# State sums of a decayed linear attention with the values as weights, and a transpose behind them

## The reference, cut to what matters

```python
Q = _xpos((x @ Wq).reshape(B, T, H, 128), 1.0)
K = _xpos((x @ Wk).reshape(B, T, H, 128), -1.0)
V = (x @ Wv).reshape(B, T, H, 64)
scores = jnp.einsum('bihd,bjhd->bhij', Q, K) * DQK ** (-0.5)
scores = scores * _decay_mask(T)[None]      # causal decay, rows normalised
out = jnp.einsum('bhij,bjhv->bihv', scores, V)
... # group norm over time, a silu gate, Wo, residual; then the feed-forward part
```

## Time and profile before

| | us |
|---|---|
| median of 3 runs | 905.84 |
| lowest and highest | 901.13, 906.43 |
| the profiled execution | 905.14 |
| its span, first to last instruction | 903.3 |
| TensorE busy in it | 858.9 |

### The profile page before, as it was taken

One profiled execution on the slowest core, in us unless ns is written; L12 is line 12 of the kernel. 1 busy time (PEld: TensorE's weight loads), 2 busy tenths in 40 slices (PEclk: granted clock), 3 DMA queues, 4 the chain that ended last, 5 costly groups with the idle time before them and its releaser, 6 DMA issues.

```text
span 903.3 us, 16221 instructions
## 1 busy us (share of the span) xinstructions
PE 858.9 (95%) x5414; PEld 399.1 (44%) x5414; DVE 657.6 (73%) x1608; ACT 588.4 (65%) x891; POOL 527.9 (58%) x481
## 2 busy tenths in 40 slices
PE   8799999999999989889899999999999999999997
PEld 3477777777688756222222222322232223222222
DVE  5666656665476687958688888878888887877774
ACT  2232322345442356868689898889979897988784
POOL 0456555544365624566857576758675767575552
PEclk9999999999999999899999999999999999999998
DMA  9500002000000097768588989788988888989773
GB/s 266 221 1 1 2 1 75 1 1 1 1 2 13 18 156 176 241 190 260 170 262 236 277 233 289 235 282 235 282 236 277 252 275 230 280 257 301 250 247 102
DMA packets 90110, 154.28 MB, mean 171 GB/s; under 512 B 30326, under 2 KB 56374, under 8 KB 89635
## 3 DMA queue, kind: packets, MB, share of 16 engines
q1 hardware_dynamic: 89542, 151.63, 55.6%
q10 hardware_dynamic: 486, 1.62, 1.2%
HBM read 138.96 MB, written 15.83 MB: 171 GB/s over the span
## 4 chain that ended last, share of the span: by engine, by line
PE 75%; ACT 10%; DVE 7%; issue 4%; POOL 2%; DMA 1%; ACTq 0%; DVEq 0%; POOLq 0%; SPq 0%
PE ps L876 17%; PE ps L813 16%; PE ps L496 5%; PE ps L852 5%; PE ps L519 3%; PE ps L590 3%; PE ps L504 3%; PE ps L643 3%; PE ps L599 3%; ACT ring L1202 2%; PE ps L529 2%; PE ps L561 2%; PE ps L581 2%; PE ps L612 2%; PE ps L664 1%
## 5 line engine op out<-in xcount | busy, mean ns | idle before, releaser
L1885 POOL TENSOR_TENSOR ring<-ring,wbc 128x512 f32<-128x512 f32 x192 | 245.0, 1278 | 151.7 <-ACT ring L1211 142.3
L1668 DVE TENSOR_TENSOR ring<-ps,ring 128x1024 f32<-128x1024 f32 x192 | 234.6, 1222 | 82.3 <-PE ps L852 55.7
L813 PE MATMUL ps<-zst,w1st 99*128 99x512 bf16 x768 | 210.9, 384 | 12.3 <-ACT ring L1202 7.3
L876 PE MATMUL ps<-ring,w2cur 128*32 128x512 f32 x1536 | 206.6, 611 | 0.0
L1202 ACT ACTIVATE ring<-ps 128x1024 f32<-128x1024 f32 x192 | 196.9, 1026 | 3.9 <-PE ps L813 3.8
L1213 ACT ACTIVATE ps<-ps 128x512 f32<-128x512 f32 x192 | 113.3, 590 | 56.5 <-PE ps L813 56.3
L1671 DVE TENSOR_TENSOR ring<-ps,wbc 128x512 f32<-128x512 f32 x192 | 130.8, 681 | 0.2 <-DMA wbc<-w_rows 0.2
L813 PEld LDWEIGHTS ps<-zst,w1st 99*128 99x128 bf16 x768 | 60.7, 97 | 137.1 <-issue 37.3
L1211 ACT ACTIVATE ring<-ps 128x512 f32<-128x512 f32 x192 | 116.6, 607 | 0.0
L1734 POOL TENSOR_TENSOR s2q<-s2q,rope 128x768 f32<-128x768 f32 x24 | 43.1, 1817 | 91.0 <-ACT s2q L1014 91.0
L852 PEld LDWEIGHTS ps<-wst,sel 32*128 32x128 bf16 x384 | 18.1, 91 | 150.7 <-DVE ring L1668 95.9
(11 more groups left out here) (181 smaller groups left out, 1297.7 us busy)
## 6 DMA issues: line engine op xcount, KB each, us to landing
wbc<-w_rows SPq DMA_DIRECT2D x192, 512.0 KB, 5.3
w2cur<-in_w SPq DMA_DIRECT2D x48, 256.0 KB, 4.9
w_parts<-wp SPq DMA_DIRECT2D x72, 64.0 KB, 3.1
zst<-z_parts SPq DMA_DIRECT2D x72, 64.0 KB, 4.3
wst<-w_parts SPq DMA_DIRECT2D x24, 128.0 KB, 4.0
z_parts<-zp SPq DMA_DIRECT2D x6, 384.0 KB, 6.3
wst<-w_parts SPq DMA_DIRECT2D x24, 96.0 KB, 3.8
out_h<-h SPq DMA_DIRECT2D x12, 192.0 KB, 5.4
```

Source lines behind the costliest of these rows:

```text
L813: return pe.matmul(bank(to), w1st[0:99, 4 * a + j, col:col + P], zst[0:99, (i // 2) % 2, j, :], start=True, stop=True)
L876: mm = pe.matmul(bank(YBANK, 0, 512, 32 * j, 32 * j + 32), w2cur[:, n, j, :], ring[:, (4 * g + j) % RING, :], start=False, stop=(n == 7 an ...
L1668: dve.tensor_tensor(v, ps[:, WBANK * 512:WBANK * 512 + 1024], v, ALU.mult).then_inc(s["duo_done"], 1)
L1885: pool.tensor_tensor(ring[:, slot, :], ring[:, slot, :], wbc[:, g % 4, 1, :], ALU.mult).then_inc(s["tri_done"], 1)
```

## The change

It concerns pairs 0 to 4 (`flips(k)`), that is the first five chunks of batches 0 and 1. Pairs 6 to 10 keep the old way.

- `flipped_sums` takes vn (64 columns) as weights and t1k (128 columns) as what moves. There are as many matmuls as before, 12 for each pair, and two heads go to the two column halves. The result is the transposed state: partitions are two heads by 64 values, columns the 128 query-key places, for three groups of heads.
- `add_sums` keeps this transposed state in buffer 0, in place: one instruction of 384 columns for x = 0, two (128 and 256 columns) for x = 1, whose sums lie in three banks.
- `turn_state` is new on TensorE: six transposes of 128 x 128 in the trip after the one that makes the sums, behind `turn(p, 0)`.
- `keep_state` is new on ScalarE: two copies of 128 x 384 from PSUM to buffer 1 of the state, from which `outputs` reads.
- New waits: TensorE waits for these copies (flip_s) ahead of `turn(p, 1)` and of `outputs`, and for the added sums (st_out) ahead of `turn_state`. DVE waits for the copies of the pair before ahead of `add_sums`.

```diff
+            def flipped_sums(k, x):
+                pe.wait_ge(s["v_out"], 2 * k + 2)
+                pe.wait_ge(s["m"], 2 * k + 2)
+                for g in range(VP):
+                    at = (6, g * P) if x == 0 else ((6, 3 * P), (4, 3 * P), (5, 3 * P))[g]
+                    for e in range(2):
+                        mm = pe.matmul(bank(at[0], at[1], at[1] + P, e * DV, e * DV + DV), vn[:, x, 2 * g + e, :],
+                                       t1k[:, x, 2 * g + e, :], start=True, stop=True)
+                mm.then_inc(s["st_full"], 1)
+            def turn_state(k):
+                pe.wait_ge(s["st_out"], 2 * k + 2)
+                pe.wait_ge(s["xn_e"], k + 3)
+                for x in range(2):
+                    v = state[:, 0, x, :, :].rearrange("p h v -> p (h v)")
+                    for g in range(VP):
+                        mm = pe.transpose(bank(7 - x, g * P, g * P + P), v[:, g * P:g * P + P], ident[:, :])
+                    mm.then_inc(s["flipped"], 1)
...
                 if x == 1:
                     pe.wait_ge(s["kept"], 2 * k + 1)
+                    if 0 < k < CH:
+                        pe.wait_ge(s["flip_s"], 2 * k)
...
+                if last and p > 0 and flips(p - 1):
+                    turn_state(p - 1)
...
+            def keep_state(k, x):
+                act.wait_ge(s["flipped"], 2 * k + x + 1)
+                act.wait_ge(s["at_full"], 2 * k + x + 1)
+                act.copy(state[:, 1, x, :, :].rearrange("p h v -> p (h v)"), bank(7 - x, 0, HV)).then_inc(s["flip_s"], 1)
...
                 if p >= 0:
                     keep(p, 0)
+                if p > 0 and flips(p - 1):
+                    keep_state(p - 1, 0)
+                    keep_state(p - 1, 1)
...
+                if flips(k):
+                    if k > 0:
+                        dve.wait_ge(s["st_out"], 2 * k)
+                        dve.wait_ge(s["flip_s"], 2 * k)
+                    v = state[:, 0, x, :, :].rearrange("p h v -> p (h v)")
+                    w = ps[:, 4 * 512:6 * 512].rearrange("p (b n) -> p b n", b=2)[:, :, 3 * P:4 * P]
+                    u = v[:, P:3 * P].rearrange("p (b n) -> p b n", b=2)
...
+                    elif x == 0:
+                        dve.tensor_tensor(v, bank(6, 0, HV), v, ALU.add).then_inc(s["st_out"], 1)
+                    else:
+                        dve.tensor_tensor(v[:, 0:P], bank(6, 3 * P, 4 * P), v[:, 0:P], ALU.add)
+                        dve.tensor_tensor(u, w, u, ALU.add).then_inc(s["st_out"], 1)
+                    return
```

More of the change, by code:

```diff
@@ L186, in fused_layer @@
                  "st1 st2 ln_var ln_std ln_done xn_d xn_t xn_e "
-                 "q_full k_full v_full g_full rq rk sq mq aq ak v_out g_out turned kept sc m st_full st_out at_full o_out dchain "
+                 "q_full k_full v_full g_full rq rk sq mq aq ak v_out g_out turned kept sc m st_full st_out flipped flip_s at_full o_out dchain "
                  "gn_in gn_m gn_dev gn_v gn_var gn_std gn_done yn yn_dve h_b yg_e yg_o yg_t wo_s res "
@@ L202, in sums_before, with flips @@
             return 2 * (k - k // CH)
+        def flips(k):
+            return k < CH - 1
         def attention_over(eng):
@@ L591, in heads @@
                 mm.then_inc(s["sc"], 1)
+            def flipped_sums(k, x):
[15 more added lines that the diff above has]
+                    mm.then_inc(s["flipped"], 1)
             def sums(k, x):
+                if flips(k):
+                    flipped_sums(k, x)
+                    return
                 pe.wait_ge(s["v_out"], 2 * k + 2)
@@ L614, in outputs @@
                             else:
-                                mm = pe.matmul(o, state[:, k % 2, x, 2 * g + e, :], qT[:, (2 * g + e) // 3, (2 * g + e) % 3 * 2 + x, :],
+                                mm = pe.matmul(o, state[:, 1 if k < CH else k % 2, x, 2 * g + e, :], qT[:, (2 * g + e) // 3, (2 * g + e) % 3 * 2 + x, :],
                                                start=False, stop=True)
@@ L1369, in add_sums @@
                     dve.wait_ge(s["at_full"], 2 * (k - 1) + x + 1)
+                if flips(k):
+                    if k > 0:
[4 more added lines that the diff above has]
+                    u = v[:, P:3 * P].rearrange("p (b n) -> p b n", b=2)
+                    if k == 0 and x == 0:
+                        dve.tensor_copy(v, bank(6, 0, HV)).then_inc(s["st_out"], 1)
+                    elif k == 0:
+                        dve.tensor_copy(v[:, 0:P], bank(6, 3 * P, 4 * P))
+                        dve.tensor_copy(u, w).then_inc(s["st_out"], 1)
+                    elif x == 0:
[3 more added lines that the diff above has]
+                        dve.tensor_tensor(u, w, u, ALU.add).then_inc(s["st_out"], 1)
+                    return
                 new = state[:, (k + 1) % 2, x, :, :].rearrange("p h v -> p (h v)")
```

## The result

The changed kernel takes 901.21 us in the median of 20 runs (899.5 to 903.92), the kernel before 905.35 in 20 runs (901.13 to 908.0). The ratio is 0.9955, with a 95% interval of 0.9943 to 0.9967: 4.1 us less, with 3.0 to 5.2 in the interval. The forecast was 3.3 less. The profiled execution took 901.19 us, with a span of 899.4 against 903.3.

A forecast was written before the change was run, and what follows sets the result against it. TensorE, busy without a gap, was taken to bound the kernel. Sums saved 6.95 us, transposes added 3.65, other engines' work nothing: -3.3 us, from the median 905.84 to 902.5 us, range 898.5 to 907.0.

The forecast's parts named there:

- What bounds the kernel: From 45 to 165 us TensorE is busy for 120.00 of 120.00 us; other engines' work costs nothing until TensorE waits.
- The price of the new sums: Sums with 64-column weights, pairs 0 to 4: 1.43 us instead of 2.82, saving 1.39 a pair, 6.95 in all.
- The price of the transposes: Six transposes for each of five states, trips 2 to 6: 0.73 us each, 3.65 in all, on TensorE's path.
- the ends of the sum: Net saving over the five pairs with the lower and upper prices of sums and transposes: 3.6 and 3.0 us.
- The range: Whole kernel, 898.5 to 907.0 us: scatter of earlier runs, upward taking in the cases that end at 905.8.
- No new wait: Changed trips: TensorE waits nowhere anew, with 1.3 us left ahead of the values, 1.1 to 1.3 ahead of `turn(p, 1)`.
- The halves in turn: New sums on TensorE: column halves do not overlap, sums cost 2.81 us a pair, kernel 909.4; chance 0.04.
- The copies late: ScalarE's copies of the state hold up `turn(p, 1)`; 0.66 us beyond the margin the time is 905.8; chance 0.04.
- The clock: Twelve transposes in a row lower TensorE's clock in five trips: 16.6 us cost, time 919; chance 0.03.
- Given back later: The feed-forward part, bound by other chains in places, loses the 3.3 us in a longer wait: 905.8; chance 0.05.

The follow-up runs named there:

- transposes left out: The changed kernel without the six transposes and two copies of each of the five states, and without the waits for them: 897.18 us, 0.9915 of before.
- copies twice: The changed kernel with each ScalarE copy of the state from PSUM made two times, with a wait between: 902.71 us, 0.9967 of before.
- one half alone: The changed kernel with both heads of a couple writing their sums to the lower column half: 907.5 us, 1.0019 of before.
- late release: The changed kernel with DVE's first rotation of keys waiting for the sums of both x in the changed pairs: 902.7 us in one execution.
- five copies: The changed kernel with each ScalarE copy of the state made five times, with a wait between: 923.55 us, 1.0199 of before.

## Why the prediction was right

**What bounds the kernel.** Right: TensorE alone. Both halves of this were tested. Work taken from TensorE came off the trips one for one (transposes left out), and work on ScalarE cost the trips nothing up to its margin (copies twice).

**The price of the new sums.** I took 1.43 us from two rows for L612 and L615; it was 1.36, below my ends of 1.39 and 1.47. The mechanism behind it, two halves side by side, was the doubtful step, and one half alone shows it. From the 2.38 times that the Trainium skill (TensorE: Matmul & The Clock Gate, Part 3: Packing small matmuls — row/col tiling) gives for three column tiles I had estimated 1.77 us as an alternative; two tiles of 64 columns with a new weight for each matmul took 1.36 here, so that measured figure stands for this shape. The rule that the Trainium skill states in the same section, that weight loads overlap with matmuls in flight only when the row group differs, isn't borne out here either: 24 weights were loaded and used in 1.36 us with both halves, and 24 records took 2.6 us with one.

**The price of the transposes.** I took 0.73 us; it was 0.65, below my ends of 0.71 and 0.75. The groups of rows 5 stand behind matmuls of another kind, and the new group stands directly behind six transposes. A group behind others of its kind pays less at its border, and I could have seen that, since 0.71 and 0.75 for equal groups were already different by their neighbours. The same may hold for the products behind the sums, shorter by 0.06 us, which I booked at nothing. These three sizes turn the 3.3 us into 5 x 0.81 + 4 x 0.06 = 4.3, less the wait of 0.12: 4.2, beside 4.1 measured in the medians, 4.1 in the changed trips of the trace and 3.9 in its whole loop. Trips 2 to 5 were shorter by 0.85 us each where I had written 0.66. All three errors are small and go the same way, so the saving in the trace lies outside the 3.0 to 3.6 that I gave as the ends of the sum. Of the 1.3 us between the forecast time, 902.5, and the measured 901.21, 0.8 are this, and 0.5 come from the start: I counted from 905.84, the median of three runs, and that of twenty is 905.35.

**The range.** It was 898.5 to 907.0, so wide that the time of a change that brings nothing would have lain in it too. That the change gains something rests on the interval (0.9943 to 0.9967) and the trips. I had also written that under 1% can't be told from no change; with twenty runs of each kernel, 0.45% can.

**No new wait.** Right in trips 2 to 5: 1.2 us were left ahead of the values, 1.3 forecast, and 1.5 ahead of `turn(p, 1)`, 1.1 to 1.3 forecast. Wrong in trip 1. I had worked out the margin in trip 3 only and written "no new wait" for all. The earlier trace rows had shown what differs: in the first pair only 1.47 us of products stand between the sums and the values, not 2.78. The cost was 0.12 us of idle time, and late release shows how near the edge this was.

**The rivals.** The halves in turn: refuted by the trace. Its time (909.4) lay near to what the hand-made case gave, 907.5. The copies late: refuted, and the margin measured from both sides. The clock: twelve transposes in a row left the granted clock at 1.00 from 45 to 165 us. The Trainium skill (TensorE: Matmul & The Clock Gate, Part 4: PE-mode transpose) says that transposes count differently for the gate; in rows of twelve, 1.36 us long, between matmuls, nothing of that showed here. Where the clock did fall was behind waits of TensorE of 2.6 us, in the kernel with five copies. Given back later: no, the span is 3.9 us shorter and 3.85 of that were there at the end of the loop.

## What to carry to other kernels

When an engine is busy without a gap, price an exchange of its work by the distance between starts of the nearest group of the same shape, and mind the neighbours: groups of six equal transposes took 0.65, 0.71 and 0.75 us, by what stood ahead of them. If a product has 64 columns on one side, look whether it can be the weight: with work for both column halves here it took half the time of the other way round (1.36 against 2.82 us for 12 matmuls), and turning the result back cost 0.65 us, less than half of what was won. Work out the margin for each kind of trip of a loop, the first one too, and when a change is extended to more trips look for the wait that swallows it: here moving one DVE instruction freed it.

## What the runs showed of the hardware

- Records for one column half start between earlier records of the other half. With three matmuls in a row for the same half the sums and products took 4.35 us instead of 4.08, with all in one half 5.38. Within one half records start 0.11 us apart.
- After 2.6 us without work TensorE's granted clock was 0.56 over the next 3.9 us in trip 2 (a mixture of 1.2 and 2.4 GHz), and 0.57, 0.63 and 0.70 over the 3.8 us from the second turning in trips 3 to 5. The wait cost 4.3 us where 2.6 were seen as idle, in these four trips; in the fifth the clock stayed at 1.00.
- The start scatters by the clock: the same group of L500, 8 records behind a wait, took 2.82 us in the trace of the change and 5.46 in that of the five copies (after 2.85 us of waiting in both), and 4.51 before, after 3.96. The first turning of the keys began at 41.7 us in the earliest trace and at 46.3 in the latest. That scatter is as large as what the change brought. That is why stretches behind the start tell more here than single times.
